# A block of per-tile statistics issued later in each step of an attention sweep (pre-norm transformer block, 8 cores)

## What is computed

```python
q = softmax((h @ Wq.T + bq) @ Wfq.T + bfq, axis=-1)      # h = layernorm(x)
k = softmax((h @ Wk.T + bk) @ Wfk.T + bfk, axis=-1)
v = h @ Wv.T + bv
scores = einsum('bhsd,bhtd->bhst', q, k)                 # 16 heads of 64
probs  = scores / sum(scores, axis=-1)
x = x + einsum('bhst,bhtd->bhsd', probs, v)
x = x + ffn(layernorm(x))    # act_quant to 8 bits, weights rounded to -1, 0, 1
```

## Time and profile before

| | us |
|---|---|
| median of 2 runs (lowest, highest) | 2174.81 (2172.21, 2177.41) |
| the profiled execution | 2170.33 |
| its span on the slowest core (core 3) | 2168.8 |
| spans of the other cores | 2149.3 to 2168.5 |

### The profile page before, as it was taken

The page is one execution under the profiler, slowest core; times in us unless marked ns, Lnnn a source line. Parts: engine busy times, 40 slices in busy tenths (PEclk is TensorE's granted clock), DMA queues, the critical chain, the costliest instruction groups (busy, mean ns, idle before and its releaser), DMA issues.

```text
span 2168.8 us, 17569 instructions; the slowest of 8 cores (2149.3 to 2168.8 us)
## 1 busy us (share of the span) xinstructions
PE 1318.0 (61%) x5801; PEld 550.9 (25%) x5801; DVE 805.6 (37%) x1323; ACT 698.1 (32%) x657; POOL 215.1 (10%) x44
## 2 busy tenths in 40 slices
PE   0062567777863454446714667775777577339999
PEld 0021122223321111112201223332333233104444
DVE  0020234334445777776412434443444433101111
ACT  0000024335433565552021554445454554200000
POOL 0100000000014555553000000000000000000000
PEclk9996878887876777667856878888888888659999
DMA  8724026555435656661197122111211120566664
GB/s 104 96 44 68 20 107 239 207 184 222 162 134 194 226 222 224 245 252 68 39 191 153 44 61 71 44 44 44 87 44 44 44 74 20 108 115 143 145 156 130
DMA packets 309193, 261.31 MB, mean 120 GB/s; under 512 B 262704, under 2 KB 262832, under 8 KB 305840
## 3 DMA queue, kind: packets, MB, share of 16 engines
q10 hardware_dynamic: 144384, 132.13, 21.0%
q1 hardware_dynamic: 160224, 117.56, 17.5%
q0 software_dynamic: 4496, 10.50, 3.7%
HBM read 159.50 MB, written 69.21 MB: 105 GB/s over the span
## 4 chain that ended last, share of the span: by engine, by line
PE 51%; DVE 17%; DMA 13%; ACT 6%; SPq 4%; ACTq 3%; issue 3%; DVEq 2%; POOLq 0%
PE pbA L1026 11%; PE pbV L1035 10%; PE pbV L557 7%; PE pbV L1181 5%; DVE sq_scr L338 5%; PE pbA L557 5%; PE pbA L1181 5%; DVE stat L345 4%; DMA wdT<-s_dq 3%; DMA wfqT<-s_wfq 3%; PE pbA L252 3%; ACTq L68 3%; ACT tq L1077 3%; DMA xt_buf<-x_own 3%; ACT hqb L1081 2%
## 5 line engine op out<-in xcount | busy, mean ns | idle before, releaser
L1026 PE MATMUL pbA<-wgT,aq2T 128*128 128x512 bf16 x1024 | 270.6, 411 | 213.3 <-ACT aq2T L997 189.7
L1035 PE MATMUL pbV<-wuT,aq2T 128*128 128x512 bf16 x1024 | 259.5, 398 | 34.9 <-DMA wuT<-s_uq 34.9
L523 POOL TENSOR_TENSOR pwq<-ppb,pwq 128x4096 bf16<-128x4096 bf16 x24 | 201.5, 8417 | 537.5 <-ACT pwq L510 537.5
L1049 DVE SCALAR_TENSOR_TENSOR hmid<-pbV,smal,silu_b 128x512 f32<-128x512 f32 x128 | 96.0, 750 | 415.1 <-PE pbV L1035 340.6
L1026 PEld LDWEIGHTS pbA<-wgT,aq2T 128*128 128x128 bf16 x1024 | 103.2, 103 | 352.9 <-issue 251.6
L557 PE MATMUL pbA<-wckT,xrT 128*128 128x512 bf16 x512 | 169.4, 490 | 30.9 <-DVE xrT L622 30.9
L1181 PE MATMUL pbA<-wdT,hqT 128*128 128x512 bf16 x512 | 124.9, 395 | 73.1 <-DMA wdT<-s_dq 73.1
L1041 ACT ACTIVATE silu_b<-pbA,smal 128x512 f32<-128x512 f32 x128 | 88.1, 688 | 197.1 <-PE pbA L1026 176.6
L1035 PEld LDWEIGHTS pbV<-wuT,aq2T 128*128 128x128 bf16 x1024 | 104.7, 102 | 174.4 <-issue 66.4
L557 PE MATMUL pbV<-wvT,xrT 128*128 128x512 bf16 x512 | 147.4, 440 | 0.0
L374 PE MATMUL pbtr<-identb,negrm_bf 128*1 128x128 bf16 x32 | 7.7, 240 | 203.5 <-DVE negrm_bf L371 203.5
(11 more groups left out here) (132 smaller groups left out, 1272.5 us busy)
## 6 DMA issues: line engine op xcount, KB each, us to landing
pchunk<-wg ACTq DMA_DIRECT2D x16, 2048.0 KB, 10.5
pchunk<-wu ACTq DMA_DIRECT2D x16, 2048.0 KB, 10.5
pchunk<-wd ACTq DMA_DIRECT2D x16, 2048.0 KB, 10.0
xt_buf<-x_own SPq DMA_DIRECT2D x32, 512.0 KB, 4.4
s_hq<-hqb SPq DMA_DIRECT2D x16, 1024.0 KB, 6.6
xt_buf<-x_oth SPq DMA_DIRECT2D x16, 512.0 KB, 7.3
s_gq<-pwq SPq DMA_DIRECT2D x8, 1024.0 KB, 8.2
s_uq<-pwq SPq DMA_DIRECT2D x8, 1024.0 KB, 10.5
```

The costliest lines, as they stand in the source:

```text
L523: vW = p.op("gpsimd", lambda e, SGP=SGP, PWQ=PWQ: e.tensor_tensor(PWQ, SGP, PWQ, op=ALU.add), [("cAC", prep2_ac[k])], "cGP", 1)
L1026: vG = pe(lambda e, c=c, oc=oc, gp=gp, s=s: e.matmul(gp[:, 0:512], aq2T[:, s * D + c * 128:s * D + (c + 1) * 128], wgT[:, c * DI + 512 * o ...
L1035: vU = pe(lambda e, c=c, oc=oc, up_=up_, s=s: e.matmul(up_[:, 0:512], aq2T[:, s * D + c * 128:s * D + (c + 1) * 128], wuT[:, c * DI + 512 ...
L1049: e.scalar_tensor_tensor(hmid[:, oc * 512:(oc + 1) * 512], up_[:, 0:512], smal[:, sm + 6:sm + 7], silu_b[:, ss * 512:(ss + 1) * 512], op0= ...
```

## The change

`emit_next_tile_stats(t)` is called in another place of the tile: no longer between K's products and K's maximum, but behind the K·V products, ahead of the part on Q's exponential. All instructions that it issues move with it, on every engine and queue: the x load, nine instructions and an accumulator read on VectorE, two on ScalarE, one transpose on TensorE. Their number, their operands and their waits remain.

```diff
         vK = emit_proj(pbA, XRT, wckT, ROW["wcks"], ROW["bfk"], t,
                        [("cDV", vXRT)] + pbA_free)
-        emit_next_tile_stats(t)
         vNM = dv(lambda e, s=s: e.reduce_max(
             nmax[:, s:s + 1], pbA[...], axis=AX, negate=True),
             waits=[("cPE", vK)])
...
                 waits=[("cAC", vEK), ("cDV", vS2)] if pr == 0 else (),
                 inc=(pr == NPAIR - 1))
+
+        emit_next_tile_stats(t)
 
         if t < TQ:
             vNMq = dv(lambda e, s=s: e.reduce_max(
```

## The result

| | before | changed kernel |
|---|---|---|
| median, us | 2176.5 | 2184.7 |
| ratio to before, 95% interval | | 1.0046 (1.0035 to 1.0058) |
| profiled execution, us | 2170.33 | 2179.77 |
| span of the slowest core, of core 3 | 2168.8, 2168.8 | 2178.2, 2175.4 |

In some executions the cores of one die show a lower granted clock and the time is longer; the ratio leaves these out. The time is 0.46% longer: no change by the 2% bound, and 8 us in itself, which the interval tells apart from nothing. The forecast was 2192 us in a range of 2161 to 2213. Three terms of 16 to 32 us stand behind the small sum.

The account below looks back on a forecast made before the run. No engine is full, so the order of the work decides. Tiles 0 to 14 +20, 15 to 26 −29, 27 to 31 +26 sum to +17 us; on the shown median, 2192 us (+0.8%), range 2161 to 2213.

Parts of the forecast that it names:

- the rival with the cast not held: Tiles 15 to 26: L645 is not held by the adds, −1.54 us per pair, total 2174 us; chance 0.27.
- Stage A, Q's maximum (+33): Tiles 0 to 14: Q's maximum waits behind the statistics, +2.22 us per tile net of V's earlier start, +33 us.
- Stage A, late x (−19.4): Tiles 0 to 14: V's wait where x arrives late disappears, −19.4 us, not counting the wait ahead of tile 0.
- Stage A, low clock (+6): Tiles 0 to 14: after longer TensorE idle the next K stays longer at 1.2 GHz, +6 us (bounds nothing to 15).
- Stage B, L645 held: Tiles 15 to 26: the eight-element cast L645 is held to the adds' end, about 5.5 us; chance 0.55.
- The argument by xr's rate: For L645 held: xr (L610), 0.75 us for 1024 elements, moves more than one per cycle, so uses a second path.
- The rival with L640 held: Tiles 15 to 26: V's scaling L640 also runs only behind the adds, +15 us, 2207 us; chance 0.08.
- the adds at 7.94 each and the restart after them: Tiles 15 to 26: a pair of adds takes 15.88 us, the first sign follows 4.33 later; loop 27.86 instead of 29.40.
- a new wait in a shorter loop: Rival, tiles 15 to 26: a late weight chunk or store keeps the loop at 29.4 us, total 2206; chance 0.05.
- Tail (+26): Tiles 27 to 31, no Q: nothing covers the statistics, 20.6 us per tile, four tiles 82.4 against 56.5, +26 us.
- What follows (0): Everything after the sweep over 32 tiles: not touched by the change, so no term in the sum.

Follow-up runs that it names:

- early-x kernel: Kernel before, with the x load of tile t+2 issued in tile t behind the copy to xrT, ahead of the eqT store: 2153.1 us, ratio 0.9895.
- experiment 1: Changed kernel, with the eight-element cast of the reciprocal (L644) moved from VectorE to ScalarE: 2163.2 us, ratio 0.9946 to the kernel before.
- experiment 8: Kernel before, with statistics late only in tiles 15 to 26, the reciprocal's cast on ScalarE and the x load early: 2100.4 us, ratio 0.9666.
- experiment 5: Second run, on another chip, of the kernel before with statistics late only in tiles 27 to 31: ratio 1.0122 (first run 1.0153).
- experiment 7: Kernel before, with the eight-element cast of the reciprocal moved from VectorE to ScalarE, run twice: ratio 0.9946, then 0.9954.

## Why the prediction was right, point by point

The forecast of no change held, by the mechanism given, with the likeliest time 7 us too long (2192 against 2185). As a change it was +17 us, and +8 came. That the time stayed within 2% is no test of the mechanism: the rival with the cast not held forecast 2174 us, no change either. The test is in the parts, and there every wait came where it was put; only the price of the low clock did not. Each of the three sums was too long, by 4.4, 3.0 and 1.6 us on core 3, 9 us together. The prediction took 2% for about what a measurement of this kernel can tell; the interval here is 0.2% wide. The starts of K, V, Q's maximum and the next xr, tile by tile on core 3, price the terms of stage A; the early-x kernel serves as the state with neither late x nor late statistics. Mean of tiles 1 to 14, us:

| | xr to K | K to V | V to Q's maximum | from there to next xr | tile |
|---|---|---|---|---|---|
| before | 2.84 | 7.80 | 9.07 | 4.91 | 24.62 |
| changed | 2.87 | 6.21 | 11.19 | 5.28 | 25.55 |
| before, x early | 2.84 | 6.50 | 8.77 | 4.96 | 23.07 |

- **Stage A, Q's maximum (+33)**: 11.19 instead of 8.77 behind V, and V 0.29 sooner: +2.13 a tile over the early-x state, +32 for 15 tiles. As predicted.
- **Stage A, late x (−19.4)**: K to V holds 1.30 us of it in the mean, and V to Q's maximum another 0.30. The second part was not in the sum: behind a long wait for x V's products ran partly at the low clock, in tiles 1, 5 and 8 (in tile 1 the first eight take 3.17 us instead of 1.90, and V to Q's maximum is 10.0 to 10.4 us instead of 8.77). With x early the whole of stage A is 20.8 us shorter on this core, tile 0 included, for the 19.4 of the waits.
- **Stage A, low clock (+6)**: mis-sized and in the wrong place. K to V is 6.21 us, against 6.18 in the early-x state without the transpose's 0.32, so K pays nothing in the mean, though tile 11 alone, 6.94, looks like the upper bound. What pays is the way from Q's maximum to the next xr, 0.32 a tile, 4.5 us in all, and of that 0.2 are the eight transposes of Q's exponential: 1.01 us in all but one of these tiles, behind 2.91 us of idle TensorE, against 0.61 to 1.01 behind 2.11 us with x early. Sum 32 − 20.8 + 4.5 = +15.7; measured +15.6 on core 3. The three are cut from the same starts, so that they add up is no proof; that each has its sign and size is.
- **Stage B, L645 held**: the step on which most hung, with a chance of 0.55. It is held, 5.04 us (5.5 were given), and experiment 1 shows what it costs. The argument by xr's rate stays untested, for no run has xr beside an add. The Trainium skill, "SBUF — State Buffer", section "Who interferes with whom", says that a cast in a two-port mode and a GpSimd instruction lock each other out as wholes, and that an instruction with one SBUF input outside those modes does not contend. The trace agrees on both: L644 held 5.04 us, L639 not at all beside the same add (1.28), and L335 not beside an add in the earlier trace rows and in experiment 1 (1.21). That L644 runs in such a mode is concluded from its holding; nothing else here shows it. The rival with L640 held falls with the same lines.
- **Stage B, the adds at 7.94 each and the restart after them**: a pair takes 15.82 us (15.88 predicted, 16.79 before), the adds start 7.63 us behind the sign (7.65), and the next sign follows 4.18 us behind their end (4.33), since L335 starts 0.05 us before the add's recorded end and not 0.1 behind it. The loop is 27.64 (27.86). On core 3 the tiles up to the first sign of tile 16 gave −10.7 (−9.7), nine loops −15.9 (−13.9), the end −5.5 (−5.3): −32.0 for −29. Three small amounts, all to the same side; the largest is the nine-fold 0.2 of the loop.
- **Stage B, a new wait in a shorter loop**: none came, the loop is 27.6 us on all cores, and that rival falls too. At 26.3 us its mechanism begins to show: in experiments 1 and 8 the second sign waits on some cores for a store, up to 1.1 us at a time, which is why the loops there are 26.41 and 26.36 in the mean and not 26.3.
- **Tail (+26)**: +23.9, on core 3 +24.4. A tile is 20.2 us, not 20.6. K at the low clock throughout, "as after every idle", was overdone: K to V takes 6.19 us, not the 7.02 of tile 31 before, and xr to K takes 2.83, not 2.45. The other two terms (4.53 and 6.64) came as given. In tile 31 0.9 us more came up, which the sum did not have.
- **What follows (0)**: +2.8 in the mean of the cores. The sum took an untouched part to be unchanged; by experiments 5 and 7 such a part moves by up to 8 us with the kernel ahead of it. For a sum of terms that cancel to 10 us this is the largest uncertainty, and the prediction did not name it.

## What to carry to other kernels

A block that is moved in a written-out order should be priced separately in each stage, by what covers it there: here the same move was worth −32 us under the GpSimd adds, +16 where another engine waited behind it (some +36, but for the late x that it hid) and +24 where nothing lay over it, and the profit was in applying it only to the first. Before a small instruction on VectorE is put beside GpSimd work, look at whether it can be locked out: length says nothing, for a cast of eight elements, 0.18 us by itself, cost 1.25 us of every loop. And a wait that a move removes by accident (the late x, 20 us) is better removed by itself.

## What the runs showed of the hardware that was not expected

- **An add is lengthened by a long VectorE instruction with two SBUF inputs, not by a one-element one.** In the second run of experiment 7, core 3, the statistics meet the adds one instruction later than before: L338 still runs when the first add starts, and L345 and then L349, both with one element and two inputs, are held by one add each:

```profile
806.25 1.23 DVE L338 SCALAR_TENSOR_TENSOR sq_scr<-xt_buf 128x1024 f32<-128x1024 f32 x1
...
807.83 7.47 DVE L345 TENSOR_TENSOR stat<-stat 128x1 f32<-128x1 f32 x1
815.39 7.77 DVE L349 SCALAR_TENSOR_TENSOR stat<-stat 128x1 f32<-128x1 f32 x1
```

```profile
806.62 8.66 POOL L523 TENSOR_TENSOR pwq<-ppb,pwq 128x4096 bf16<-128x4096 bf16 x1 [13.18 <-ACT pwq L510]
...
815.24 7.90 POOL L523 TENSOR_TENSOR pwq<-ppb,pwq 128x4096 bf16<-128x4096 bf16 x1
```

  The first add takes 8.66 us instead of 7.94, with L338 in its first 0.86 us. The second, ahead of which L345 had its turn, takes 7.90, no more than with nothing in between (7.91 in the changed kernel). In the kernel before it is the second add that is long, 8.9 us, and there it is L338 that gets in ahead of it. In the kernels with late tiles 0 to 14 and 27 to 31 L338 runs as the very first add starts, and that add takes 8.84 and 8.55 us.
- **An untouched part takes another time by what lies ahead of it**: the first feed-forward half took 715 to 727 us over the kernels of this study, within 7 us on a kernel's cores and again in its second run (726.3 and 727.0; 714.9 and 715.5). For the most part it is how soon behind each pause the clock of 2.4 GHz is granted: TensorE is busy 503.3, 498.8 and 494.9 us in it where it takes 727.0, 720.6 and 714.9.
